# Layer 0 of a four-layer cross-attention stack: softmax weights applied to the raw memory rows, with one folded projection behind them

## The reference

```python
memory_proj = einsum('bme,de->bmd', memory, W_mem)              # 128 -> 256
scores = einsum('bnd,bmd->bnm', hidden, memory_proj) / sqrt(256)
attn = softmax(scores)
context = einsum('bnm,bmd->bnd', attn, memory_proj)
gate = sigmoid(concat([hidden, context]) @ W_gate.T + b_gate)
x = rmsnorm(hidden + gate * context, norm_w)
```

## Time and profile before

| what | us |
|---|---|
| median of three runs | 2259.29 |
| lowest and highest run | 2249.55, 2263.94 |
| the profiled execution | 2255.95 |
| its span, first to last instruction | 2254.1 |
| last scatter of layer 0 issued | 154.03 |
| first load of layer 1 issued | 157.10 |

### The profile page before, as it was taken

How to read it: one execution, slowest core, us unless ns; L and a number is a source line. 1 busy time by engine, 2 the same in 40 slices (tenths; PEclk the granted TensorE clock), 3 DMA queues, 4 the chain that set the end, 5 groups by cost and what they waited for, 6 DMA issues and landing times.

```text
span 2254.1 us, 63424 instructions
## 1 busy us (share of the span) xinstructions
PE 2092.3 (93%) x23904; PEld 1683.3 (75%) x23905; DVE 1375.4 (61%) x2831; ACT 1142.4 (51%) x2595; POOL 813.3 (36%) x1045
## 2 busy tenths in 40 slices
PE   7978999889979997999999979997999989979998
PEld 4646777655659997788888859986777756659997
DVE  6756888656753333666666655554888757763333
ACT  4765666455653332544544535354666546663332
POOL 1654444278632221111121112224444336642222
PEclk9989999989989998999999989998999989989999
DMA  7425444120131113100000010004444320011111
GB/s 230 122 82 161 134 136 129 52 86 23 29 106 58 57 61 101 37 2 2 2 2 3 2 39 19 26 22 130 137 132 136 110 77 28 28 44 61 56 58 35
DMA packets 105988, 155.08 MB, mean 69 GB/s; under 512 B 24100, under 2 KB 82289, under 8 KB 105617
## 3 DMA queue, kind: packets, MB, share of 16 engines
q1 hardware_dynamic: 87952, 95.39, 13.7%
q0 software_dynamic: 16560, 55.23, 7.6%
q10 hardware_dynamic: 1232, 1.05, 0.2%
HBM read 86.69 MB, written 56.28 MB: 63 GB/s over the span
## 4 chain that ended last, share of the span: by engine, by line
PE 80%; DVE 8%; issue 2%; ACT 2%; DMA 1%; another core or an unknown queue 1%; POOL 1%; POOLq 0%; DVEq 0%; ACTq 0%; SPq 0%
PE ps_all L2394 4%; PE ps_all L2396 4%; PE ps_all L2395 4%; PE ps_all L1626 3%; PE ps_all L1598 3%; PE ps_all L1189 3%; PE ps_all L1175 3%; PE ps_all L1207 3%; PE ps_all L1968 2%; PE ps_all L2419 2%; PE ps_all L2421 2%; PE ps_all L2420 2%; PE ps_all L2404 2%; PE ps_all L1612 2%; PE ps_all L1157 2%; PE ps_all L1642 2%
## 5 line engine op out<-in xcount | busy, mean ns | idle before, releaser
L403 POOL TENSOR_TENSOR a_probs<-a_probs,a_sm 128x1024 f32<-128x1024 f32 x32 | 60.9, 1903 | 345.5 <-DVE a_sm L398 345.5
L1370 POOL TENSOR_TENSOR pool_w<-s_qkt,const 128x512 f32<-128x512 f32 x128 | 131.5, 1049 | 88.8 <-ACT s_qkt L1304 88.8
L2394 PE MATMUL ps_all<-f_wh,f_xh 128*128 x396 | 154.0, 389 | 5.3 <-DVE f_xl L2540 5.3
L1748 POOL TENSOR_TENSOR c_kx<-c_qkt,const 128x512 f32<-128x512 f32 x128 | 130.9, 1042 | 76.2 <-ACT c_qkt L1691 75.7
L2396 PE MATMUL ps_all<-f_wl,f_xh 128*128 x396 | 148.4, 375 | 0.0
L2395 PE MATMUL ps_all<-f_wh,f_xl 128*128 x396 | 148.4, 375 | 0.0
L2100 ACT ACTIVATE self_w<-ps_all,a_q_bias 128x256 f32<-128x256 f32 x128 | 53.8, 471 | 183.4 <-PE ps_all L1944 183.4
L2535 DVE SCALAR_TENSOR_TENSOR f_h<-ps_all,rstd,f_act_g 128x688 f32<-128x688 f32 x66 | 61.7, 934 | 135.2 <-PE ps_all L2396 135.2
L374 DVE TENSOR_REDUCE s_mx<-ps_all 128x8 f32<-128x512 f32 x128 | 82.5, 687 | 75.7 <-PE ps_all L1175 75.7
L2458 ACT ACTIVATE f_act_g<-ps_all,rstd 128x688 f32<-128x688 f32 x66 | 55.2, 837 | 134.9 <-PE ps_all L2396 134.9
L1699 ACT ACTIVATE c_pt<-ps_all 128x512 f32<-128x512 f32 x128 | 69.5, 594 | 104.6 <-PE ps_all L1612 95.1
(11 more groups left out here) (339 smaller groups left out, 6874.5 us busy)
## 6 DMA issues: line engine op xcount, KB each, us to landing
qkv_sorted<-pool_w SPq DMA_DIRECT2D x66, 392.0 KB, 2.4
pool_w<-pool_w SPq DMA_DIRECT2D x128, 68.0 KB, 2.2
s_x_in<-x_sorted SPq DMA_DIRECT2D x66, 128.0 KB, 2.3
f_x_in<-x_sorted SPq DMA_DIRECT2D x66, 128.0 KB, 2.0
x_res<-x_sorted SPq DMA_DIRECT2D x66, 128.0 KB, 2.2
x_sorted<-x_res POOLq DMA_DIRECT2D x1, 4224.0 KB, 17.6
l_rows<-in_x SPq DMA_DIRECT2D x32, 128.0 KB, 2.3
x_res<-in_x SPq DMA_DIRECT2D x32, 128.0 KB, 3.1
```

The source lines that it names most:

```text
L1370: ins = nc.gpsimd.tensor_tensor(kx[:, p % 2, c], qkt[:, p % 2, 2 + c].rearrange("p (b k) -> p b k", b=2).unsqueeze(2) .broadcast_to([P, 2, ...
L1748: ins = nc.gpsimd.tensor_tensor(kx[:, p % 2, b], qkt[:, p % 2, 1, b * S:b * S + S].unsqueeze(1).broadcast_to([P, RH, S]), const[:, C_H8X:C ...
L2394: nc.tensor.matmul(bank, x_high, wh[:, w_at], start=(c == 0), stop=False)
```

## The change

The softmax weights multiply the raw memory rows first (`mix`: 128 columns instead of 512), the transposed result is copied to SBUF (`mix_copy`, `mem_t`, 128 columns, placed behind `gate_x_bias`), and the 512-column projection `w_both` is applied to that (`context`). `memory`, `memory_copy` and the buffers `both` go. The context is no longer copied out of PSUM with its 1/sum (`context_copy`, `mc` go): `add_gated` reads it from PSUM, the factor 0.5 sits in the context half of `w_both`, and 1/sum is applied in the addition to x. `context`, `gate_z`, `tanh_`, `add_gated`, `square`, `rstd_` and `normed` move one step later. The memory rows are now read by `mix`, so `rows` has six buffers and `load(p)` waits for `mix(p-6)`.

```diff
 # TensorE
-                    def memory(p):
-                        if v_ok.due(p):
-                            pe.wait_ge(v_ok.handle, v_ok.at(p))
-                        nc.tensor.matmul(ps_d[:], xt[:, p % X, 2 * P:3 * P], w_both[:], start=True, stop=True) \
-                            .then_inc(v_pe.handle, 1)
+                    def mix(p):
+                        pe.wait_ge(pt_ok.handle, pt_ok.at(p + 1))
+                        if c_ok.due(p):
+                            pe.wait_ge(c_ok.handle, c_ok.at(p))
+                        nc.tensor.matmul(ps_d[:, 0:P], rows[:, p % R, D:D + DC], pt[:, p % 2], start=True, stop=True) \
+                            .then_inc(c_pe.handle, 1)
                     def context(p):
-                        pe.wait_ge(pt_ok.handle, pt_ok.at(p + 1))
-                        pe.wait_ge(v_ok.handle, v_ok.at(p + 1))
-                        if mc_ok.due(p - 1):
-                            pe.wait_ge(mc_ok.handle, mc_ok.at(p - 1))
-                            pe.wait_ge(z_ok.handle, z_ok.at(p - 1))
+                        pe.wait_ge(c_ok.handle, c_ok.at(p + 1))
+                        if gated_ok.due(p - 1):
+                            pe.wait_ge(gated_ok.handle, gated_ok.at(p - 1))
-                        nc.tensor.matmul(out_banks[p % 2][:], pt[:, p % 2], both[:, p % M], start=True, stop=True) \
+                        nc.tensor.matmul(out_banks[p % 2][:], mem_t[:, p % 2], w_both[:], start=True, stop=True) \
                             .then_inc(pv_pe.handle, 2)
-                    for p in range(PAIRS + 1):
+                    for p in range(PAIRS + 2):
                         if has(p):
                             scores(p)
                         if has(p - 1):
                             probs_t(p - 1)
                         if has(p + 1):
                             query(p + 1)
-                            memory(p + 1)
                         if has(p + 2):
                             xt_(p + 2)
+                        if has(p - 2):
+                            context(p - 2)
                         if has(p + 1):
                             gate_x(p + 1)
                         if has(p - 1):
-                            context(p - 1)
+                            mix(p - 1)
 # SyncE: ring of the raw rows, R = 4 -> 6, freed by mix instead of by the transpose
-                            sp.wait_ge(xt_pe.handle, xt_pe.at(p - R + 1))
+                            sp.wait_ge(c_pe.handle, c_pe.at(p - R + 1))
 # ScalarE: context_copy removed; tanh_ and square one step later
-                        if has(p - 2):
-                            tanh_(p - 2)
-                            context_copy(p - 2)
+                        if has(p - 3):
+                            tanh_(p - 3)
...
-                        if has(p - 2):
-                            square(p - 2)
+                        if has(p - 3):
+                            square(p - 3)
 # VectorE
-                    nc.vector.tensor_copy(w_both[:, 0:D], w_mem_t[:]).then_inc(wq_ok.handle, 1)
+                    nc.vector.tensor_scalar(w_both[:, 0:D], w_mem_t[:], 0.5, None, ALU.mult).then_inc(wq_ok.handle, 1)
-                        nc.vector.tensor_copy(both[:, p % M], ps_d[:]).then_inc(v_ok.handle, 1)
+                        nc.vector.tensor_copy(mem_t[:, p % 2], ps_d[:, 0:P]).then_inc(c_ok.handle, 1)
-                        nc.vector.scalar_tensor_tensor(gated[:], th[:, p % 2], 1.0, mc[:, p % 2], ALU.add, ALU.mult) \
-                            .then_inc(gated_ok.handle, 1)
+                        nc.vector.scalar_tensor_tensor(gated[:], th[:, p % 2], 1.0, out_banks[p % 2][:, 0:D],
+                                                       ALU.add, ALU.mult).then_inc(gated_ok.handle, 1)
-                        nc.vector.scalar_tensor_tensor(x_tile(p), gated[:], 0.5, x_tile(p), ALU.mult, ALU.add) \
+                        nc.vector.scalar_tensor_tensor(x_tile(p), gated[:], col(inv, p), x_tile(p), ALU.mult, ALU.add) \
 # VectorE's loop: gate_z(p - 3), max_(p), the table work of the step, add_gated(p - 3),
 # inverse(p), gate_x_bias(p + 1), mix_copy(p - 1), normed(p - 4); memory_copy(p + 1) removed
-                        if has(p + 1):
-                            memory_copy(p + 1)
...
+                        if has(p - 1):
+                            mix_copy(p - 1)
+                        if has(p - 4):
+                            normed(p - 4)
 # GpSimd
-                        if has(p - 2):
-                            rstd_(p - 2)
+                        if has(p - 3):
+                            rstd_(p - 3)
...
-                    for p in range(PAIRS - 2, PAIRS):
-                        put_sorted(p)
+                    put_sorted(PAIRS - 1)
```

More of the change, by code:

```diff
@@ L192, in build @@
         weights_in = [count(f"weights_in{u}", 16) for u in range(2)]
-        rows_in_sem = [count(f"rows_in{u}", 16) for u in range(4)]
-        gx_pe, gx_ok, mc_ok, z_ok, th_ok, gated_ok = (
-            count(name) for name in ("gx_pe", "gx_ok", "mc_ok", "z_ok", "th_ok", "gated_ok"))
+        rows_in_sem = [count(f"rows_in{u}", 16) for u in range(6)]
+        c_pe, c_ok = count("c_pe"), count("c_ok")
+        gx_pe, gx_ok, z_ok, th_ok, gated_ok = (
+            count(name) for name in ("gx_pe", "gx_ok", "z_ok", "th_ok", "gated_ok"))
         stored = count("stored", 16)
@@ L468, in layer0 @@
                 w_mem_t, w_gate, bias, w_norm, w_mem = w_l0
-                R, X, M = 4, 3, 3
+                R, X = 6, 3
                 rows = ob("rows", [P, R, D + DC])
@@ L473, in layer0 @@
                 w_both = ob("w_both", [P, 2 * D])
-                both = ob("both", [P, M, 2 * D])
+                mem_t = ob("mem_t", [P, 2, P])
                 gx = ob("gx", [P, 4, D])
@@ L484, in layer0 @@
                 pt = ob("pt", [P, 2, P])
-                mc = ob("mc", [P, 2, D])
                 z = ob("z", [P, 2, D])
@@ L621, in _ @@
                     pe.wait_ge(wq_ok.handle, wq_ok.at(2))
-                    memory(0)
                     gate_x(0)
                     shapes_t()
-                    for p in range(PAIRS + 1):
+                    for p in range(PAIRS + 2):
                         if has(p):
@@ L675, in pt_copy @@
                         act.wait_ge(pt_pe.handle, pt_pe.at(p + 1))
-                        if pv_pe.due(p - 1):
-                            act.wait_ge(pv_pe.handle, pv_pe.at(p - 1))
+                        if c_pe.due(p - 1):
+                            act.wait_ge(c_pe.handle, c_pe.at(p - 1))
                         nc.scalar.activation(pt[:, p % 2], ps_p[:, 0:P], ACT.Copy).then_inc(pt_ok.handle, 2)
[L680 to L685, removed]
                     def tanh_(p):
@@ L741, in max_, with mix_copy @@
                         nc.vector.tensor_scalar(col(neg, p), col(mx, p), -SCALE, None, ALU.mult).then_inc(sub_ok.handle, 2)
[L743 to L746, removed]
-                        nc.vector.tensor_copy(both[:, p % M], ps_d[:]).then_inc(v_ok.handle, 1)
+                    def mix_copy(p):
+                        dve.wait_ge(c_pe.handle, c_pe.at(p + 1))
+                        if pv_pe.due(p - 1):
+                            dve.wait_ge(pv_pe.handle, pv_pe.at(p - 1))
+                        nc.vector.tensor_copy(mem_t[:, p % 2], ps_d[:, 0:P]).then_inc(c_ok.handle, 1)
                     def gate_x_bias(p):
@@ L912, in _ @@
                     shapes()
-                    memory_copy(0)
                     gate_x_bias(0)
-                    for p in range(PAIRS + 4):
-                        if has(p - 2):
-                            gate_z(p - 2)
+                    for p in range(PAIRS + 5):
+                        if has(p - 3):
+                            gate_z(p - 3)
                         if has(p):
                             max_(p)
-                        if has(p + 1):
-                            memory_copy(p + 1)
                         if p == 0:
@@ L935, in _ @@
                             masks()
-                        if has(p - 2):
-                            add_gated(p - 2)
+                        if has(p - 3):
+                            add_gated(p - 3)
                         if has(p):
@@ L941, in _ @@
                             gate_x_bias(p + 1)
-                        if has(p - 3):
-                            normed(p - 3)
+                        if has(p - 1):
+                            mix_copy(p - 1)
+                        if has(p - 4):
+                            normed(p - 4)
                 @block.gpsimd
@@ L981, in keep_context @@
                             .then_inc(ctx_ok.handle, 1)
-                    for p in range(PAIRS + 2):
+                    for p in range(PAIRS + 3):
                         if has(p):
@@ L1000, in layer0 @@
                 close(2, wq_ok)
```

(4 more changed lines are left out.)

1 line of the change is left out of this document (removed).

## The result

| what | before | after |
|---|---|---|
| median of 20 runs, us | 2256.44 | 2243.77 |
| lowest and highest run | 2249.47, 2263.94 | 2235.82, 2255.64 |
| the profiled execution | 2255.95 | 2237.92 |
| its span | 2254.1 | 2236.0 |
| last scatter of layer 0 issued | 154.03 | 145.65 |

The ratio after to before is 0.9945 with an interval of 0.9931 to 0.9959, so the change takes 9 to 16 us off (12.7 between the medians); the forecast was 12.3. (It named 2247.0 as the median, counted from 2259.29, which is the median of the first three runs of the kernel before; by twenty it is 2256.44.) But layer 0 ended only 8.2 us earlier in the profiled execution, and the other 9.9 us by which its span is shorter lie in code that did not change. So layer 0 has to be read by itself, and first against its own steps.

A forecast was written before the change was run, and what follows sets the result against it. TensorE was taken to bound layer 0, at 3.88 us a step without waits. Gains of 4.4 + 1.3 + 2.2 + 4.4 + 0 = 12.3 us put the median at 2247.0, range 2238 to 2257 (90%).

The forecast's parts named there:

- TensorE's step: TensorE per step of layer 0: `memory` 0.86 us removed, `mix` 0.22 added, 3.88 to 3.25, a gain of 0.635.
- VectorE's step: VectorE's own work per step: 3.05 to 2.75 us by the smaller copy, up to 3.0 with waiting for tanh.
- The rival of VectorE or ScalarE as the bound at 3.5: Waits for tanh and exp make the step 3.5 us instead of 3.25: 2250 us in all, chance 12%.
- Steps 0 to 11: Start of layer 0 up to scores(12): gain 8.9 us without data shortage, less 4.5 of stall, so 4.4.
- the stall: Loads 6, 7 and 8 fall in the earlier fill, so their rows come late: 4.5 us, bounds 0 and 9.
- the distance of 7.4 us: Time from issuing `load(p)`, behind `mix(p-6)`, until its rows are needed: 7.4 us, down from 15.5.
- Steps 12 and 13: Two steps at TensorE's gain of 0.635 us each: 1.3 us.
- Steps 14 to 30: Steps 14 to 23, two scatters each, set by GpSimd: gain 2.2 us; steps 24 to 30 at TensorE's pace: 4.4.
- The slack: The ring `xt` lets GpSimd be late by about 1.2 us in the two-scatter steps before it costs time.
- The end: From scores(31) to the last scatter: 13.7 us against 13.4, taken as 0, bounds 1.5 shorter and 2 longer.
- Data and GpSimd take most of it back: Rival: a stall of 9 us and a stretched GpSimd copy leave a gain of 5, 2254 us; chance 23%.
- TensorE's pace everywhere: Rival: loads land in time and GpSimd's slack suffices, gain 21 us, 2238 us; chance 15%.

The follow-up runs named there:

- The padded kernel: Changed kernel plus an unused 256-column product ahead of `mix` in each step: 2246.66 us in its one run, step 3.67 us instead of 3.24.
- the kernel with all three repairs: Changed kernel with the fill in step 6, eight row buffers and scatters spread from step 12 on: median 2229.66 us, ratio 0.9905 to the kernel before.
- its copy: Unchanged copy of the changed kernel, run again for a second profile: median 2244.92 us over 12 runs, ratio 0.996 to the kernel before.
- spread scatters: Changed kernel with one scatter a step from step 9 and two in every fifth, instead of two in steps 14 to 23: median 2243.4 us, ratio 0.9939.
- masks late: Changed kernel with the four mask DMAs behind `load(13)` instead of `load(6)` and their table work in step 16: 2245.08 us, ratio 0.9958.

## Why the prediction was right, and where only by its sum

**TensorE's step** was right: 3.25, and no product waits for `mix_copy`. From `mix` to the next scores it is 0.32 (83.81 to 84.13); 0.09 of that lay ahead of the scores before too, where the trace has 0.95 from `context` to them and 0.86 is its length, so `mix` is the 0.22 of the forecast within 0.01. The padded kernel shows that this engine sets the plain steps.

**VectorE's step** was put at 2.75 and is less. Its timeline in a step with table work:

```profile
29.21 0.47 DVE L725 SCALAR_TENSOR_TENSOR l_z<-ps_all,l_inv,l_gx 128x256 f32<-128x256 f32 x1
...
29.99 1.22 DVE L869 TENSOR_TENSOR l_before_v<-l_v_up_to,l_full_l 128x1024 f32<-128x1024 f32 x1
31.12 0.42 DVE L754 SCALAR_TENSOR_TENSOR l_gated<-l_th,ps_all 128x256 f32<-128x256 f32 x1
...
32.37 0.28 DVE L738 COPY l_mem_t<-ps_all 128x128 f32<-128x128 f32 x1
...
32.96 0.48 DVE L725 SCALAR_TENSOR_TENSOR l_z<-ps_all,l_inv,l_gx 128x256 f32<-128x256 f32 x1
```

From `gate_z` to `gate_z` is 3.75 with 1.13 of table work (29.99 to 31.12) and no wait: 2.62 by itself. The copy takes 0.19 start to start, `add_gated` from PSUM 0.42 as from SBUF. The rival of VectorE or ScalarE as the bound at 3.5 is out: with the copy put back and 0.43 of waiting in every step they still follow at 3.25.

**Steps 0 to 11** is the step that failed: a gain of 4.4 was forecast and scores(12) came 0.8 later than before (67.91 against 67.09). Its parts: scores(4) at 28.78 instead of 27.3 (1.5 worse); from there to scores(12), without the stall, 28.4 us instead of 30.9 (2.5 better; in the kernel with all three repairs, which has no stall, it is 29.2, so 1.7 of this has nothing to do with the stall and goes with VectorE's shorter step, and the other 0.8 fits with table work that runs on under the stall, which is argued and not tested); the stall 10.8 instead of 4.5 (6.3 worse). The count without a stall was good: the kernel with all three repairs has scores(12) at 56.93 where 58.2 was forecast.

The stall was missed twice over. Its cause was put to the distance of 7.4 us that `load(p)` is given, and more buffers change nothing (8.15 against 8.28). With the masks out of the way that cause does appear, at 4.53 for a forecast of 4.5, but in the changed kernel the hold covers it. The mechanism is SyncE's queue: the fill left at 22.39 instead of 33.47, as forecast to within 2 us, and with the masks behind it SyncE stood 11.40 us in one issue. The prediction named the masks ("behind four mask DMAs") and had row 7 at 38.5, but priced an issue beside the fill at the 1.32 that the earlier trace rows show, where the masks had been issued 8 us before the fill, and charged only part of the lateness to TensorE. And it charged nothing for the clock that falls in such a wait, 2.3. Of the rows 6 to 8 that it expected late only row 7 was waited for.

**Steps 12 and 13**: 1.29, as forecast.

**Steps 14 to 30** were forecast to gain 6.6 and gained 7.6 (scores(14) to scores(31): 65.74 before, 58.18 after). GpSimd led later and for longer: the steps with two scatters gained 4.8 instead of 2.2, and steps 24 to 26, thought free, were led too, so the last seven gained 2.8 instead of 4.4. The prediction had named scatter steps at 3.25 as a sign that it is wrong, and seven of the ten, 14 to 20, run at 3.24 or 3.25. The slack was 3.2, not 1.2: the first scatter of a step starts 5.07 behind its scores in step 14 (79.47 to 74.40) and 8.25 in step 20 (102.11 to 93.86). Beyond it the engine's own step is 3.81; the 3.66 of the forecast is near what it is as long as nothing is stretched, 3.62 (first scatters at 83.15 and 86.77), so the price of an unstretched step was right and a new stretch came in. Timelines of GpSimd, ScalarE and VectorE, beside the earlier trace rows:

```profile
108.44 0.30 POOL L969 COPY ctx_all<-l_xt 128x128 f32<-128x128 f32 x1
...
109.73 1.24 POOL L963 DMA_INDIRECT x_sorted<-x_res,slot_i  x1 [0.19 <-issue]
...
108.85 0.49 ACT L654 ACTIVATE l_xt<-ps_all 128x384 f32<-128x384 f32 x1 [0.66 <-POOL ctx_all L969]
...
109.57 0.48 DVE L762 SCALAR_TENSOR_TENSOR x_res<-x_res,l_factor,pool_w 128x256 f32<-128x256 f32 x1 [0.57 <-POOL l_factor L954]
```

ScalarE's `xt` copy waits 0.66 for `ctx_all`, as the prediction said it would, in six steps. The copy itself is 0.30, not 0.54. The Trainium skill (SBUF — State Buffer, section Who interferes with whom) says that a VectorE instruction with two SBUF inputs contends with a GpSimd instruction that reads SBUF. By that rule, the trace agrees: `normed` (L762), the one beside the copy before, no longer lies there. In its place the first scatter of each of steps 18 to 24 has grown from 1.04 to 1.24: it starts 0.16 behind `normed`, which in six of the seven has itself waited for GpSimd's factor. The coincidence is the same in all twelve profiles: each of the 56 scatters that start 0.15 to 0.17 behind `normed` takes 1.23 or 1.24, and no other scatter has either length. That `normed` causes it is not tested, since no run moved `normed` alone.

**The end** was taken as 0 and gained 0.35, 13.07 from scores(31) to the last scatter. GpSimd:

```profile
143.09 0.18 POOL L951 TENSOR_TENSOR l_shifted<-l_power,eps 128x1 f32<-128x1 f32 x1 [0.16 <-ACT l_junk L689]
```

The last `rstd_` is 10.51 behind scores(31) (forecast 10.9), and two scatters follow.

**The sum.** In layer 0: -0.8 + 1.3 + 7.6 + 0.35 = 8.4, up to the last scatter, where 12.3 was forecast; the second profile of the same kernel has 9.9 up to the first load. By the runs after gains 9.3 to 15.6, its copy 5.2 to 13.1. So the total agrees to half a microsecond, and that is luck: of the 12.7 us between the medians layer 0's rows account for 8.2 to 9.9, and the other 2.7 to 4.4 are not explained by them. What they are is open, and the interval allows that they are none: for nine of the ten kernels that have an interval the gain of layer 0 lies inside the interval of the runs (all three repairs 20.9 in 15.8 to 26.8, spread scatters 11.4 in 8.6 to 18.9, masks late 12.6 in 5.9 to 13.1), and only for the first comparison, 8.2 against 9.3 to 15.6, a little outside. For the context copy put back it is 5.4 in -1.1 to 7.2. These intervals are also narrower than the prediction allowed for, which took 1%, 22.6 us, as what can be told from no change. "Data and GpSimd take most of it back" (2254, stall 9) was thus the rival nearest to what happened before scores(12), and "TensorE's pace everywhere" the one nearest to it in steps 12 to 20; the forecast lay between and two errors of opposite sign met.

## What to carry to other kernels

When a step moves, follow every DMA it issues into each queue and ask what is issued right behind it there: the price is set by when the fastest engine needs the next row, so the same hold cost 1.4 us in the slow kernel and 8.3 in the fast one. Check a total by its stages, at marks that both traces have, since a sum can be right with a failed term in it. A shorter step is worth its full length only after the large transfers and the bundled scatters beside it have been spread again: here that brought 11 to 13 us, by layer 0's end in the profiles (136.2 against 147.2 and 148.9), on top of what the change itself had given.

## What the runs showed of the hardware

- One DMA issue on SyncE took 11.40 us (7.44 to 11.89 in the seven profiles with this order) where four mask DMAs of 64 KB stood directly ahead of it while a fill of 4.2 MB was in flight. In all seven it ended 14.9 to 15.6 us after the fill's issue; the fill landed 17.4 after it in after. In 21 to 45 us of after 4399 of 7015 packets are under 512 bytes (297 of 3294 in the same stretch of the kernel with the masks later):

```profile
DMA packets 7015, 5.96 MB, mean 248 GB/s; under 512 B 4399, under 2 KB 5956, under 8 KB 7012
```

  Where the masks did not stand ahead of the loads, or went out long before the fill, no issue beside the fill was over 1.6; without the fill the masks took 2.68 to 5.57 for all four, and the issue behind them 0.56 to 0.61. Which resource is full in between no run here shows.
- Behind a wait of 8.28 us TensorE's granted clock was 0.50 in 41 to 47 us, behind one of 4.53 it was 0.50 in 37 to 41, behind one of 3.65 it was 0.84 in 58 to 60 and 0.50 in 60 to 62, and behind one of 1.39 it stayed at 1.00 (41 to 45).
- GpSimd's first scatter of a step took 1.04 us in most steps and 1.23 or 1.24 in each of the 56 cases in which `normed` had started 0.15 to 0.17 ahead of it; the cause is not tested.
